# Another order of TensorE, ScalarE and VectorE between the attention part and the first expert tile of a fused transformer block

## The reference

```python
h = _L0_tok_ref(x, L0_tok_W, L0_tok_b, L0_tok_class_token, L0_tok_pos_embed)
h = jnp.concatenate([h, txt], axis=1)
h = h + _L0_attn_ref(_layernorm(h, axis=-1), L0_attn_Wqk, L0_attn_bqk, L0_attn_lepe_w, L0_attn_lepe_b)
h = h + _L0_ffn_ref(_layernorm(h, axis=-1), L0_ffn_gate_w, ...)
...
        z = 1.0 / (jnp.einsum('bhnd,bhd->bhn', qh, kmean) + 1e-06)
        kv = jnp.einsum('bhnd,bhne->bhde', k_r * scale, vh * scale)
        out = jnp.einsum('bhnd,bhde->bhne', q_r, kv) * z[..., None]
...
        shared = jax.nn.silu(xt @ sw1) * (xt @ sw3) @ sw2
        _, idx = jax.lax.top_k(scores + biases, K)
        h = jax.nn.silu(jnp.einsum('td,edh->eth', xt, w1)) * jnp.einsum('td,edh->eth', xt, w3)
        y = jnp.einsum('eth,ehd->etd', h, w2)
        out = jnp.einsum('te,etd->td', comb, y) + shared
```

## Time and profile before

| | |
|---|---|
| time, median of 3 executions | 267.1 us (266.92 to 267.6) |
| time of the profiled execution | 267.63 us |
| its span, first to last instruction | 265.8 us |
| TensorE busy | 233.1 us (88%) |
| VectorE busy | 192.2 us (72%) |
| ScalarE busy | 154.9 us (58%) |
| GpSimd busy | 114.0 us (43%) |
| mean granted clock of TensorE | 0.973 of 2.4 GHz |

### The profile page before, as it was taken

One profiled execution on the slowest core, in us unless ns is written; L12 is line 12 of the kernel. 1 busy time (PEld: TensorE's weight loads), 2 busy tenths in 40 slices (PEclk: granted clock), 3 DMA queues, 4 the chain that ended last, 5 costly groups with the idle time before them and its releaser, 6 DMA issues.

```text
span 265.8 us, 5589 instructions
## 1 busy us (share of the span) xinstructions
PE 233.1 (88%) x1489; PEld 192.1 (72%) x1489; DVE 192.2 (72%) x738; ACT 154.9 (58%) x436; POOL 114.0 (43%) x121
## 2 busy tenths in 40 slices
PE   0499799999999999988879956999999999999960
PEld 0487688888888888856556635888888888887640
DVE  1532999797979797987977885766666666665884
ACT  0325458585757676774934541666666666666471
POOL 1300000064737372721744730566666666666400
PEclk9999799999999999988999997999999999999996
DMA  6999955052515201010101512223333332329566
GB/s 201 332 269 340 329 211 180 5 173 71 172 69 172 83 31 32 30 32 0 51 31 40 119 47 61 79 73 100 84 86 90 87 91 82 90 68 280 152 151 179
DMA packets 31421, 31.71 MB, mean 119 GB/s; under 512 B 4322, under 2 KB 27275, under 8 KB 30496
## 3 DMA queue, kind: packets, MB, share of 16 engines
q1 hardware_dynamic: 25960, 23.95, 30.7%
q0 software_dynamic: 3392, 6.36, 7.3%
q10 hardware_dynamic: 2040, 1.06, 1.5%
HBM read 22.82 MB, written 9.03 MB: 120 GB/s over the span
## 4 chain that ended last, share of the span: by engine, by line
PE 80%; DVE 10%; ACT 4%; ACTq 2%; issue 2%; DVEq 0%
PE bank L1565 15%; PE bank L1286 12%; PE bank L1585 9%; PE bank L1301 5%; PE bank L1574 5%; PE bank L1478 4%; PE bank L1481 3%; PE bank L1493 3%; PE bank L1374 3%; PE bank L1556 2%; PE bank L1394 2%; PE bank L1378 2%; PE bank L1300 2%; PE bank L1334 2%; PE bank L1332 2%
## 5 line engine op out<-in xcount | busy, mean ns | idle before, releaser
L777 POOL DMA_INDIRECT xs_dram<-xd,pos_i x50 | 55.4, 1107 | 85.7 <-DVE pos_i L966 72.9
L788 POOL DMA_INDIRECT y_dram<-att,goal x56 | 55.1, 983 | 38.4 <-ACT att L712 38.1
L1286 PE MATMUL bank<-wt,xp_both 128*128 128x128 f32 x288 | 38.6, 288 | 0.0
L698 ACT ACTIVATE att<-bank 128x256 f32<-128x256 f32 x56 | 21.5, 383 | 28.5 <-PE bank L1565 28.5
L1286 PEld LDWEIGHTS bank<-wt,xp_both 128*128 128x128 f32 x288 | 36.9, 201 | 1.2 <-issue 0.5
L1195 DVE CAST xsT_h<-bank 128x128 fp32r<-128x128 f32 x56 | 16.3, 291 | 26.3 <-PE bank L1556 26.3
L1585 PE MATMUL bank<-w_sb,att 128*128 x224 | 34.5, 277 | 0.0
L1585 PEld LDWEIGHTS bank<-w_sb,att 128*128 128x128 f32 x224 | 29.4, 191 | 0.4 <-issue 0.2
L1565 PE MATMUL bank<-xp_both,xsT_h 128*128 x56 | 27.3, 488 | 0.7 <-DVE xsT_l L1197 0.7
L1208 DVE TENSOR_TENSOR att<-att,bank 128x256 f32<-128x256 f32 x56 | 23.0, 411 | 1.7 <-ACT att L698 1.7
L1565 PE MATMUL bank<-xp_both,xsT_l 128*128 x56 | 22.6, 403 | 0.0
(11 more groups left out here) (200 smaller groups left out, 490.9 us busy)
## 6 DMA issues: line engine op xcount, KB each, us to landing
xp_both<-in_patches SPq DMA_DIRECT2D x7, 1152.0 KB
xs_all<-xs_dram SPq DMA_DIRECT2D x56, 64.5 KB, 1.9
xd<-y_dram SPq DMA_DIRECT2D x8, 384.0 KB, 5.1
w<-in_w SPq DMA_DIRECT2D x2, 1024.0 KB, 9.8
y_dram<-att,goal POOLq DMA_INDIRECT x56, 2.3
xs_dram<-xd,pos_i POOLq DMA_INDIRECT x50
hrow<-in_txt SPq DMA_DIRECT2D x2, 384.0 KB, 9.8
out_tokens<-hrow SPq DMA_DIRECT2D x6, 128.0 KB, 1.9
```

The source lines that it names most:

```text
L698: A(hs[q][:], bank[2 + q][:, 0:HID], ACT.Silu).then_inc(silu_done[at], 1)
L777: nc.gpsimd.indirect_dma_start(out=xs_dram[:, :], out_offset=bass.IndirectOffsetOnAxis(ap=pos_i[0:rows, j, k:k + 1], axis=0), in_=xd[0:row ...
L788: nc.gpsimd.indirect_dma_start(out=y_dram[:, :], out_offset=bass.IndirectOffsetOnAxis(ap=goal[u][:, 0:1].bitcast(I32), axis=0), in_=ys[u][ ...
L1286: M(ps[:, 0:D], xp[p][:, k, :], wt[:, k, :], start=(k == 0), stop=False)
```

## The change

No instruction is added or taken away; functions are called at other places, from the last round of the loop to the first tile. `centre_tap(G - 1)` and `tap_before(G - 1)` come earlier; on TensorE `place(G - 3)`, `turn_second(G - 2)` and `gate(G - 2)` come earlier and `mixed_rows(G - 1)` behind them; on ScalarE `norm2(G - 2)` and `columns2(G - 2)` come ahead of the table load for Silu; on VectorE the shared expert and the weight parts are spread otherwise, and `choices(G - 1)` is followed directly by `positions(G - 1)`. The core of the diff:

```diff
@@ scalar
+                if i == G - 2:
+                    centre_tap(G - 1)
...
-            centre_tap(G - 1)
+            round_w13(1)
+            queries(G - 1)
             by_turns(G - 1)
-            queries(G - 1)
-            round_w13(1)
             round_w13(2)
-            round_w13(3)
+            turned_queries(G - 1)
+            rstd2(G - 2)
             key_sums(G - 1)
-            rstd2(G - 2)
-            turned_queries(G - 1)
+            norm2(G - 2)
             inverse_log(G - 1)
             inverse(G - 1)
+            columns2(G - 2)
             act.preload_act_table(ACT.Silu)
-            norm2(G - 2)
             shared_silu(0, 0)
+            scores(G - 2)
...
+            shared_silu(2, 0)
+            round_w13(4)
             act.wait_ge(nm2_done, G)
...
-            shared_silu(2, 0)
+            shared_silu(2, 1)
             act.wait_ge(x2_turned, G)
...
-            shared_silu(2, 1)
+            round_w13(5)
@@ vector
+            tap_before(G - 1)
             attended(G - 2)
...
+            tap_behind(G - 1)
+            remainder_w13(0)
             positions(G - 3)
-            tap_behind(G - 1)
+            remainder_w13(1)
             attended(G - 1)
...
             choices(G - 2)
+            shared_add(0)
+            shared_mul(1, 0)
             dve.wait_ge(rs2_done, G)
...
+            shared_mul(1, 1)
+            positions(G - 2)
             dve.wait_ge(nm2_done, G)
...
-            positions(G - 2)
-            shared_add(0)
-            shared_mul(1, 0)
-            shared_mul(1, 1)
-            remainder_w13(2)
             remainder_w13(3)
             shared_mul(2, 0)
+            shared_mul(2, 1)
+            remainder_w13(4)
             shared_add(1)
-            shared_mul(2, 1)
             choices(G - 1)
-            shared_mul(3, 0)
             positions(G - 1)
@@ tensor
-            pe.wait_ge(s_wexp, 96)
+            place(G - 3)
             turn_queries(G - 1)
             mixed_rows(G - 2)
-            place(G - 3)
+            pe.wait_ge(s_wexp, 96)
             shared_up(0, 0)
+            pe.wait_ge(rr_done, G)
+            turn_turned(G - 1)
             sums(G - 1)
-            turn_turned(G - 1)
+            shared_up(0, 1)
             attend(G - 1)
-            shared_up(0, 1)
+            turn_second(G - 2)
+            gate(G - 2)
             mixed_rows(G - 1)
             shared_up(1, 0)
-            turn_second(G - 2)
             mixed_cls()
-            gate(G - 2)
...
+            shared_down(2)
             shared_up(3, 0)
-            shared_down(2)
             place(G - 1)
             shared_up(3, 1)
             shared_up(4, 0)
+            shared_down(3)
             shared_up(4, 1)
-            shared_down(3)
```

More of the change, by code:

```diff
@@ L1089, in _ @@
             turn(G - 1)
-            tap_before(G - 1)
             second_stats(G - 2)
@@ L1135, in _ @@
             then(V.tensor_copy(tf[:], ti[:, 1, :]))
-            shared_add(2)
+            shared_mul(4, 0)
+            shared_add(3)
+            shared_mul(4, 1)
             V.tensor_scalar(t_w[:], tf[:], float(-P), float(CAP), ALU.mult, ALU.add)
@@ L1144, in _ @@
             V.tensor_scalar(tab_r[:], t_r[:], float(E * CAP), None, ALU.min).then_inc(tab_done, 1)
-            shared_mul(4, 0)
-            shared_add(3)
-            shared_mul(4, 1)
+            shared_add(4)
+            shared_mul(5, 0)
+            shared_mul(5, 1)
+            remainder_w13(7)
             then(V.tensor_reduce(t_e[:], ge[:], AX.X, ALU.add))
@@ L1169, in _ @@
             V.tensor_tensor(by_slot[:], part[:, 0], part[:, 1], ALU.add).then_inc(top_done, 1)
-            for e in range(5, E):
-                remainder_w13(e)
-            shared_add(5)
             def weights(step):
```

27 lines of the change are left out of this document (12 added, 15 removed).

## The result

The changed kernel took 265.32 us (median of 20 executions, 264.08 to 267.87), the kernel before 267.64 us in 20 executions beside them on the same chip (266.86 to 272.28). The ratio is 0.991, 95% interval 0.988 to 0.994: about 2.3 us faster. 263.9 was forecast, and 262.4 to 266.0 as the range; the forecast gain was 3.2 (from 267.1). The profiled execution of the changed kernel took 267.57 us with a span of 265.8, as long as that of before.

A forecast was written before the change was run, and what follows sets the result against it. VectorE's own list, not the data, was taken to end last ahead of tile 0. The steps bring its split from 161.37 to 157.85, 3.5 us: 267.1 - 3.5 = 263.6, taken as 263.9 for handovers; range 262.4 to 266.0.

The forecast's parts named there:

- rival B: TensorE's clock falls at about 128.3, behind `attend(7)`, to 1.2 GHz for 3.4 us: 265.1 us, band 264.5 to 266.0; chance 0.26.
- 3: `zr` of group 7: On ScalarE, `norm2(6)` goes ahead of the denominators, so `zr` ends at 126.50 instead of 125.89: +0.6 us.
- 4: `mixed_rows(7)` behind the gate: On TensorE, `mixed_rows(7)`, queued behind the gate that ends at 127.6, is ready at 127.75: no wait, margin 0.1.
- 5: GpSimd's start of group 6: VectorE's way to `positions(6)`, which ends at 135.5; GpSimd starts at 135.8 instead of 136.12: -0.35 us.
- Step 6: TensorE's stall ahead of `shared_up(2, 1)` goes: `choices(7)` at 139.49 instead of 142.06, `positions(7)` 2.68 us earlier.
- Step 7: GpSimd's writes of group 7 start at 143.7 instead of 146.18, 2.5 us earlier; tile 0's rows there at 156.8.
- Step 8: VectorE from `positions(7)` to tile 0: 11.3 us work, 1.8 waits; split at 157.85 instead of 161.37, gain 3.5 us.
- behind the split: From VectorE's split of tile 0 to the end of the span: nothing changes, 104.4 us stay.
- E: TensorE's clock fall at 118.1 may be missing in an execution: 1.0 us more won, 262.9 us; chance 0.10.
- D: TensorE stays at 1.2 GHz from 128 through `gate(7)`: slower, 270.4 us; chance 0.05.
- C: Gain not passed on in steps 6 and 8: about 266.7 us, chance 0.12; sign: VectorE idle over 2.5 between 142 and 156.
- The table load: On ScalarE, 1.28 us without further drain; with the skill's drain of about 1380 ns the gain would be 2.6.

The follow-up runs named there:

- second series: The changed kernel unaltered, run again beside the kernel before: 266.21 us in 9 executions, ratio 0.994 (0.990 to 0.997).
- second trace of before: The kernel before, unaltered, profiled a second time: 267.06 us in one execution.
- head_only: The changed kernel with the old order behind `choices(7)`, the new order only up to there: 265.49 us, ratio 0.987 to the kernel before.
- norm_behind: The changed kernel with `norm2(6)` put back behind `inverse(7)` on ScalarE, still ahead of the table load: 269.36 us in one execution.
- mid_old: The changed kernel with VectorE's `shared_add(0)`, `shared_mul(1, 0)` and `shared_mul(1, 1)` put back behind `positions(6)`: 266.67 us in one execution.

## Why the prediction was right, and where it was off

**The sign and the mechanism** were right: the time is within the range, the steps that were to bring the gain brought it, and no rival took it. But 265.3 is not in the band that the summed chain was given (263.2 to 264.5); it lies in that of rival B, which did not come about, so that the range holds it is in part luck. 3.2 us were forecast and 2.3 measured (1.7 in the second series), and part of the distance to 263.9 is that before itself takes 267.6 in twenty executions and not the 267.1 of three. The size of the gain in the tail was forecast as 3.5 and measured as 2.86, step by step, from `exps_most(7)` on and against the second trace of before:

| step | forecast | measured |
|---|---|---|
| 3: `zr` of group 7 | +0.6 | 9.53 - 8.93 = +0.60 |
| 4: `mixed_rows(7)` behind the gate, margin 0.1 | no wait | none; the gate itself waited 0.75 |
| 5: GpSimd's start of group 6 | -0.35 | 19.42 - 19.70 = -0.28 |
| 6: `choices(7)` | -2.57 | 23.23 - 25.63 = -2.40 |
| 6: `positions(7)` | -2.68 | 26.47 - 28.74 = -2.27 |
| 7: first write of group 7 | -2.5 | 27.49 - 29.75 = -2.26 |
| 8: split of tile 0 | -3.5 | 42.08 - 44.94 = -2.86 |
| behind the split, at like clock | 0 | 105.02 - 104.42 = +0.60 |

*Step 6* lost 0.41 of its 2.68. The stall went as described, from 1.72 to 0.20, and not to nothing. Then `positions(7)` waited 0.93 for `place(7)`, a handful of tiny products that stand on TensorE behind `shared_down(2)` and `shared_up(3, 0)`: its last one began at 143.86, whereas what VectorE hands it was ready at 143.1. I had given the way from `choices(7)` to `positions(7)` 3.00, and it took 3.24. I priced `place(7)` by its own length and not by what stands ahead of it on its engine.

*Step 8* was 0.25 short: 15.36 forecast from `positions(7)` to the split, 15.61 measured. The waits in the changed profile are 0.18, 0.77, 0.69 and 0.40, 2.04 in all, where I had 1.8; the place of each was right (the Silu, `shared_down(3)`, `shared_up(4, 1)`, `shared_down(5)`). 0.41 + 0.25 is the 0.66 that was missing. (The terms of the forecast, 155.6 + 0.84 + 1.27, make 157.7; 157.85 was used, so the sum by its own terms is 3.66.)

*Step 7* was right in its read: 1.9 was taken, and the median read took 1.8 to 2.0 in every trace, single ones up to 4.5. It had GpSimd's own queue as what sets the start of group 7, with under 0.5 of idle time; in the trace GpSimd idles 0.80 and it is `positions(7)` that ends last. *Step 8's order of lateness* was right too (VectorE, then TensorE, 0.65 ahead of it in the forecast and 0.8 to 0.9 in the traces). What it didn't say is that the new order of the tail was not needed for this: head_only ends 0.13 earlier with three of the four weight parts where they were. The prediction read the 1.80 of three weight parts in the earlier trace rows as what held tile 0 up. It is what ended last, but most of the tail moves forward as a whole once `choices(7)` does, and what the new order of the tail saves in waits behind `positions(7)` (2.04 instead of 2.46 in head_only: 0.25, 1.00 and 1.21 for the transpose) it pays with `shared_mul(3, 0)` (0.47), which now stands behind `positions(7)` as well.

*Behind the split* the prediction put the change at nothing ("104.4 us stay"). At like clock 0.3 to 0.6 more is left there with the new order, as shown above. I put it at nothing because the code behind the split is the same; this one term missed by about as much as all the steps of the tail together.

**The rivals.** *B* did not come about: the clock in the changed kernel was 1.00 from 128 to 143 in both of its traces, while in norm_behind, with a wait of 1.93 there instead of 0.75, it fell, and stayed down for 6.8 us and not the 3.4 that I had priced at 1.2. *E*, the missing fall at 118, happened in both traces of the changed kernel. I had treated it as a small chance on top of the gain. It is missing in one of two traces of before as well, and it is there in those of norm_behind and mid_old, which have the new order ahead of it, so it is no part of the change; it was worth 1.26, where I had 1.0. *D* did not come about, and *C* not as a loss, but the sign that I had set for C was there: VectorE's waits of 0.93, 0.18, 0.77 and 0.69 between 142 and 156 make 2.57, over the 2.5 I had named, and with the 0.40 at 157 it is 2.97. The sign left little room: the forecast itself had 1.8 of waits there, behind 0.7 for `place(7)`. *The median:* the tail's 2.86 would make 267.64 - 2.86 = 264.8. With the 0.60 behind the split taken off it is 2.26 and 265.4; measured were 265.3 in one series and 1.7 below before (267.93 to 266.21) in the other. That fits, but the 0.60 is from one trace of each kernel at like clock. Whether executions with more low clock at the first tiles also play a part isn't shown. Where the mean clock is 0.976, three executions of the changed kernel took 264.5 to 265.2 and seven of before 265.6 to 267.3, about 1.9 apart on average; at 0.961 it is 267.6 to 268.1 against 268.9 to 269.9. What makes the clock fall once or twice at tile 0 in the same kernel stays open.

The table load: in the stretch from 105 to 170 of all traces a load begins 0.01 to 0.03 behind the end of the operation ahead of it and takes 1.28, and an operation behind it that waits for nothing else begins at most 0.09 behind its end (in the rows above the copy ends at 127.55 + 0.46 and the load begins at 128.03). The rule of the Trainium skill (ScalarE: Activation LUTs, What ACT_TABLE_LOAD costs) of a further drain is not seen here either.

## What to carry to other kernels

Compare two traces from the last instruction that both kernels share, not from the start of the span: here the 2.9 us won in the tail can't be seen in spans that differ by as much through TensorE's clock. But look behind the last point that you compare as well: a part of what was won ahead of it can be lost there (0.3 to 0.6 us here). Ahead of the last phase of a kernel, look for the earliest wait that everything behind it inherits (1.72 us at one product, because VectorE had its order the wrong way round), and test the halves of such a change apart: here reordering what comes behind that wait was worth nothing on top. A tiny product that another engine waits for costs what stands ahead of it on TensorE, so place it by that.

## What the runs showed of the hardware

Which falls of TensorE's clock to 1.2 GHz take place differs between executions of the same instructions: in the fourteen traces the stretch at about 30 us had 3.42, 6.8 or 10.25 us at 1.2 GHz, and each further fall of 3.4 us, there or elsewhere, moved what follows by 1.0 to 1.7 us. The profiled execution of the changed kernel had 10.24 + 6.82 + 3.58 = 20.6 us of it; the last of these lies behind 262, where TensorE has nothing left to do and it costs nothing, so a mean clock tells less than where the low stretches lie. The executions spread from 264 to 268 us, more than the change is worth, and the six of twenty with mean clocks of 0.961 to 0.964 are the six slowest (266.6 to 267.9, the others 264.1 to 266.5). The Trainium skill (TensorE: Matmul & The Clock Gate, Part 1: The HAM clock gate) says that the number of slow products differs from run to run, which the traces bear out, and that the warm-up costs less than 1% of a typical span. By that, as an estimate, it would be under 2.7 us here. A first stretch of 3.42 us, which can cost at most half of that, 1.7, stays within it; one of 10.25 put `exps_most(7)` some 2.8 us later than one of 3.42 (117.8 against 115.0 on average), and the extremes of the spread between executions (264.08 to 267.87) are 1.4% apart. Five products that nobody reads, in TensorE's waits ahead of the first tiles, went with a clock of 1.00 there in three traces of three (of the eleven others one had that), and the kernels with them had the three shortest medians of the study, 263.1 to 264.3. Nine of their 18 executions had a mean clock of 0.980 or more; none of the others on record did. That the products bring it is thus well supported; how they do it isn't shown.
